# A fused attention and feed-forward kernel on one Trainium2 core: the order of the last four work units, the PSUM banks they use, and the last batch's feed-forward by halves

## The reference

```python
# x: (16, 256, 256) f32; 16 query heads, 4 key/value heads, head size 128
x = x + attn(layernorm(x))   # mask: k <= q and (k < 4 or k >= q - 31)
#   q = x @ wq.T; k = x @ wk.T; v = x @ wv.T; softmax(q k / sqrt(128)) v; then @ wo.T
x = x + ffn(layernorm(x))
#   w_q = round(weight / w_scale), per output row; x_q = round(x / x_scale), per token
#   y = (x_q @ w_q.T) * x_scale * w_scale + bias
```

## Time and profile before

| | us |
|---|---|
| median of three runs | 634.7 (633.99 to 635.71) |
| the profiled execution | 634.63 |
| its span, first to last instruction | 632.8 |
| PE busy | 599.3 (95%) |
| DVE busy | 544.8 (86%) |
| ACT busy | 399.7 (63%) |
| POOL busy | 307.8 (49%) |

### The profile page before, as it was taken

One profiled execution on the slowest core, in us unless ns is written; L12 is line 12 of the kernel. 1 busy time (PEld: TensorE's weight loads), 2 busy tenths in 40 slices (PEclk: granted clock), 3 DMA queues, 4 the chain that ended last, 5 costly groups with the idle time before them and its releaser, 6 DMA issues.

```text
span 632.8 us, 18148 instructions
## 1 busy us (share of the span) xinstructions
PE 599.3 (95%) x7589; PEld 529.5 (84%) x7589; DVE 544.8 (86%) x1084; ACT 399.7 (63%) x631; POOL 307.8 (49%) x302
## 2 busy tenths in 40 slices
PE   5759999999999999999999999999999999999983
PEld 4547888889898988989898888989898888989872
DVE  5876899989898988989898998989898998988885
ACT  5676766566666666666666666667666666665740
POOL 1142445464565546455554646456554745535440
PEclk9989999999999999999999999999999999999996
DMA  9931401213040311203040221304030120304000
GB/s 295 352 103 20 116 1 49 55 35 85 3 117 2 86 34 46 73 15 105 1 120 2 67 52 37 83 9 112 3 96 24 53 68 20 99 1 118 3 18 34
DMA packets 33841, 41.31 MB, mean 65 GB/s; under 512 B 3936, under 2 KB 24416, under 8 KB 33760
## 3 DMA queue, kind: packets, MB, share of 16 engines
q1 hardware_dynamic: 33616, 40.02, 22.9%
q10 hardware_dynamic: 144, 0.13, 0.1%
HBM read 10.26 MB, written 4.19 MB: 23 GB/s over the span
## 4 chain that ended last, share of the span: by engine, by line
PE 87%; DVE 7%; ACT 3%; issue 1%; POOL 1%; DMA 1%; POOLq 0%; SPq 0%; ACTq 0%
PE ps L551 26%; PE ps L429 25%; PE ps L456 7%; PE ps L396 7%; PE ps L405 6%; PE ps L512 5%; PE ps L533 4%; PE ps L534 4%; PE ps L384 1%; PE ps L578 1%; DVE WoT L1008 1%; DVE Qs L892 1%; PE ps L566 1%; PE ps L336 1%; DMA X<-in_L_attn_x 1%
## 5 line engine op out<-in xcount | busy, mean ns | idle before, releaser
L429 PE MATMUL ps<-xT,WqT 128*128 128x256 f16 x1536 | 178.2, 273 | 2.0 <-DVE WqT L1008 1.3
L551 PE MATMUL ps<-WoT,pool 128*128 128x256 f16 x1536 | 178.0, 273 | 0.2 <-DVE pool L916 0.2
L429 PEld LDWEIGHTS ps<-xT,WqT 128*128 128x128 f16 x1536 | 147.0, 98 | 19.1 <-issue 3.0
L551 PEld LDWEIGHTS ps<-WoT,pool 128*128 128x128 f16 x1536 | 147.5, 98 | 16.4 <-DVE pool L916 0.3
L1203 POOL TENSOR_TENSOR small<-E,rr 128x576 f32<-128x576 f32 x63 | 72.6, 1152 | 99.8 <-DVE rr L911 99.8
L775 ACT ACTIVATE pool<-ps 128x512 f16<-128x512 f32 x128 | 69.5, 595 | 81.7 <-PE ps L534 81.6
L1209 POOL TENSOR_TENSOR PP<-small,PP 128x576 f16<-128x576 f32 x63 | 80.9, 1284 | 68.2 <-ACT PP L768 68.2
L735 ACT ACTIVATE Qs<-ps 128x576 f16<-128x576 f32 x128 | 82.4, 644 | 43.6 <-PE ps L429 43.6
L1195 POOL TENSOR_TENSOR Sm<-Sm,mx 128x576 f32<-128x576 f32 x64 | 73.7, 1152 | 54.2 <-DVE mx L902 52.9
L892 DVE TENSOR_TENSOR Qs<-ps,Qs 128x576 f16<-128x576 f32 x128 | 92.6, 724 | 3.2 <-ACT Qs L735 3.0
L916 DVE SCALAR_TENSOR_TENSOR pool<-ps,pool 128x512 f16<-128x512 f32 x128 | 81.8, 680 | 0.8 <-ACT pool L775 0.8
(11 more groups left out here) (110 smaller groups left out, 888.0 us busy)
## 6 DMA issues: line engine op xcount, KB each, us to landing
VW<-Vn SPq DMA_DIRECT2D x48, 120.0 KB
big<-Vn SPq DMA_DIRECT2D x48, 120.0 KB
X<-in_L_attn_x SPq DMA_DIRECT2D x16, 256.0 KB, 7.7
VW<-VW SPq DMA_DIRECT2D x16, 256.0 KB, 3.2
big<-big SPq DMA_DIRECT2D x16, 256.0 KB, 3.4
out<-pool SPq DMA_DIRECT2D x15, 256.0 KB, 3.6
big<-in_L_attn_wq SPq DMA_DIRECT2D x4, 512.0 KB, 7.6
pool<-in_L_attn_wo SPq DMA_DIRECT2D x4, 512.0 KB, 9.1
```

The source lines that it names most:

```text
L429: a = pe.matmul(banks[BANK_Q[f]][:, j * 256:j * 256 + 256], WqT[:, k, wl, h * 128:h * 128 + 128], xT[:, b % 2, k, xl, :], start=(n == 1), ...
L551: a = pe.matmul(banks[BANK_OUT][:, t * 256:t * 256 + 256], OT[:, p, ol, h, t * 128:t * 128 + 128], WoT[:, 4 * g + h, wl, :], start=first, ...
```

## The change

Nothing changes in the loop except that `out_proj` of unit 59 leaves its last pass. Behind the loop:

- PE: after the scores of 62 come the queries of 63 and only then `pv` of 60; `out_proj` of 59 stands behind the scores of 63; the transposes of 63 stand directly behind those of 62.
- PSUM: `pv` of units 61 and 63 writes to the queries' banks 0 and 1. The last batch's `out_proj` writes its second row tile to bank 3, so that each tile has a bank; its matmuls go tile by tile, and in unit 63 each tile signals for itself. The feed-forward of batches 13 to 15 uses banks 6, 2 and 4.
- DVE: the last batch's residual, statistics, normalisation, quantisation and output go by tiles of 128 rows. The output of batch 14 and both additions of the bias leave DVE.
- ACT: two scaled copies make batch 14's output, and the last transpose is evacuated by halves.
- POOL: it takes both additions of the bias to x, the multiplication of batch 14's output by the weight scales and its last addition, and the reciprocal roots by tiles.

```diff
@@ -242,16 +243,32 @@
-def o_view(j):
-    return banks[BANK_O[j]][:, :].rearrange("p (h q) -> p h q", h=4), slice(128 * j, 128 * j + 128)
-def f_bank(b):
-    return BANK_KV if b == B - 1 else BANK_F
+def o_bank(u, j):
+    return (BANK_Q if u in (NU - 3, NU - 1) else BANK_O)[j]
+def o_view(u, j):
+    return banks[o_bank(u, j)][:, :].rearrange("p (h q) -> p h q", h=4), slice(128 * j, 128 * j + 128)
+def out_view(b, t):
+    if b == B - 1:
+        return banks[(BANK_OUT, BANK_F)[t]][:, 0:256]
+    return banks[BANK_OUT][:, t * 256:t * 256 + 256]
+def xq_view(b, t):
+    bank = {B - 2: BANK_PT, B - 1: (BANK_KV, BANK_O[0])[t]}.get(b, BANK_F)
+    return half(bank, BF16)[:, 0:512].rearrange("p (k t) -> p k t", k=2)[:, :, t * 128:t * 128 + 128]
+def fm_view(b, t):
+    bank = {B - 3: BANK_KV, B - 2: BANK_PT, B - 1: (BANK_KV, BANK_O[0])[t]}.get(b, BANK_F)
+    return banks[bank][:, t * 256:t * 256 + 256]
...
-    return {NU - 3: BANK_KV, NU - 1: BANK_KV}.get(u, BANK_PT)
+    return BANK_KV if u == NU - 3 else BANK_PT
@@ -314,10 +331,10 @@
-    sp.wait_ge(f_z, 2)
+    sp.wait_ge(f_zp, 2)
...
-    sp.wait_ge(f_z, 3)
+    sp.wait_ge(f_z, 1)
@@ -504,7 +521,7 @@
-            pe.wait_ge(pt_ok, u - 1)
+            pe.wait_ge(pt_ok, u)
@@ -520,7 +537,13 @@
             pe.wait_ge(vw2[j][b % 2], 16 * (b // 2 + 1))
-        if u:
+        if u == NU - 3:
+
+            pe.wait_ge(q_l, 2 * (NU - 1) + j + 1)
+        elif u > NU - 3:
+
+            pe.wait_ge(o_l, 2 * u + j - 3)
+        elif u:
@@ -543,12 +566,26 @@
+        if b == B - 1:
+            if g == 0:
+                pe.wait_ge(s_m, NU)
+            for t in range(2):
+                for h in range(4):
+                    for n, (ol, wl) in enumerate(PAIRS):
+                        a = pe.matmul(out_view(b, t), OT[:, p, ol, h, t * 128:t * 128 + 128], WoT[:, 4 * g + h, wl, :],
+                                      start=(g == 0 and h == 0 and n == 0), stop=(g == KV - 1 and h == 3 and n == 2),
+                                      skip_group_check=True)
+                if t == 0 and g == KV - 1:
+                    a.then_inc(out_ps, 1)
+            a.then_inc(out_ps, 1)
+            return
...
-                    a = pe.matmul(banks[BANK_OUT][:, t * 256:t * 256 + 256], OT[:, p, ol, h, t * 128:t * 128 + 128],
+                    a = pe.matmul(out_view(b, t), OT[:, p, ol, h, t * 128:t * 128 + 128],
@@ -557,26 +594,45 @@
-            pe.wait_ge(f_y, 2 * b)
-        elif b < B - 2:
+            pe.wait_ge(pt_ok, NU)
+        else:
...
-        v = half(f_bank(b), BF16)[:, 0:512].rearrange("p (k t) -> p k t", k=2)
-        for k in range(2):
-            for t in range(2):
-                a = pe.transpose(v[:, k, t * 128:t * 128 + 128], xq[:, t, k * 128:k * 128 + 128], idb[:, :])
+        for t in range(2):
+            for k in range(2):
+                a = pe.transpose(xq_view(b, t)[:, k, :], xq[:, t, k * 128:k * 128 + 128], idb[:, :])
...
-        if b < B - 2:
-            pe.wait_ge(s_m, 4 * b + 11 if b < B - 3 else NU)
+        if b < B - 3:
+            pe.wait_ge(s_m, 4 * b + 11)
+        elif b == B - 3:
+            pe.wait_ge(pt_ok, NU - 2)
...
-                a = pe.matmul(banks[f_bank(b)][:, t * 256:t * 256 + 256], xqT[:, k, t * 128:t * 128 + 128],
-                              WfT[:, k, :], start=(k == 0), stop=(k == 1))
+                a = pe.matmul(fm_view(b, t), xqT[:, k, t * 128:t * 128 + 128], WfT[:, k, :], start=(k == 0), stop=(k == 1))
+        a.then_inc(fm_ps, 1)
+    def ffn_last(t):
+        pe.wait_ge(f_xq, B + t)
+        if t == 0:
+            pe.wait_ge(f_y, 2 * (B - 2))
+        else:
+            pe.wait_ge(o_l, 2 * (NU - 1))
+        for k in range(2):
+            a = pe.transpose(xq_view(B - 1, t)[:, k, :], xq[:, t, k * 128:k * 128 + 128], idb[:, :])
+        a.then_inc(ft_ps, 1)
+        pe.wait_ge(f_t, B + t)
+        for k in range(2):
+            a = pe.matmul(fm_view(B - 1, t), xqT[:, k, t * 128:t * 128 + 128], WfT[:, k, :], start=(k == 0), stop=(k == 1))
@@ -659,7 +715,7 @@
-        if back:
+        if back and t < NU - 3:
@@ -669,29 +725,30 @@
     scores(u)
+    q_fill(u + 1, 0)
+    q_fill(u + 1, 1)
     pv(u - 2, 0)
     pv(u - 2, 1)
-    q_fill(u + 1, 0)
-    q_fill(u + 1, 1)
     p_transpose(u - 1)
     scores(u + 1)
-    out_proj(u - 2)
-    ffn_mm(B - 3)
+    out_proj(u - 3)
     pv(u - 1, 0)
     pv(u - 1, 1)
+    ffn_mm(B - 3)
+    out_proj(u - 2)
     p_transpose(u)
+    p_transpose(u + 1)
     pv(u, 0)
...
     out_proj(u - 1)
-    p_transpose(u + 1)
     pv(u + 1, 0)
...
     ffn_mm(B - 2)
-    ffn_t(B - 1)
-    ffn_mm(B - 1)
+    ffn_last(0)
+    ffn_last(1)
@@ -754,8 +811,22 @@
-        act.activation(xqT[:, :, :], half(f_bank(b), BF16)[:, 0:512].rearrange("p (k t) -> p k t", k=2),
-                       ACT.Copy).then_inc(f_t, 1)
+        src = bass.AP(ps, 512 * (BANK_PT if b == B - 2 else BANK_F), [[4096, 128], [1, 256]]).bitcast(BF16)
+        act.activation(xqT[:, :, :], src.rearrange("p (k t) -> p k t", k=2), ACT.Copy).then_inc(f_t, 1)
+    def ffn_last_t_evac(t):
+        act.wait_ge(ft_ps, B + t)
+        if t == 0:
+            act.wait_ge(fm_ps, B - 1)
+        act.activation(xqT[:, :, t * 128:t * 128 + 128], xq_view(B - 1, t), ACT.Copy).then_inc(f_t, 1)
+    def ffn_scaled(b):
+        act.wait_ge(fm_ps, b + 1)
+        act.wait_ge(f_o, 2 * b - 1)
+        for t in range(2):
+            act.activation(y[:, t, :], fm_view(b, t), ACT.Copy, scale=fx[b % 2][:, 2 + t:3 + t]).then_inc(f_ya, 1)
@@ -834,26 +905,28 @@
     p_high(u - 1)
+    q_high(u + 1, 0)
+    q_high(u + 1, 1)
+    exps(u)
     o_high(u - 2, 0)
     o_high(u - 2, 1)
-    q_high(u + 1, 0)
-    exps(u)
-    q_high(u + 1, 1)
     pt_evac(u - 1)
...
     o_high(u - 1, 1)
+    p_high(u + 1)
     pt_evac(u)
-    p_high(u + 1)
+    pt_evac(u + 1)
     o_high(u, 0)
     o_high(u, 1)
-    pt_evac(u + 1)
     o_high(u + 1, 0)
...
     ffn_t_evac(B - 2)
-    ffn_t_evac(B - 1)
-    act.wait_ge(f_z, 4)
+    ffn_scaled(B - 2)
+    ffn_last_t_evac(0)
+    ffn_last_t_evac(1)
+    act.wait_ge(f_z, 2)
     act.dma_start(out_v[B - 1][:, 1, :], yo[:, (B - 1) % 2, 1, :]).then_inc(out[(B - 1) % 2], 16)
@@ -952,29 +1025,51 @@
-    def with_bias(b):
-        dve.wait_ge(ld_b, 16)
-        dve.wait_ge(f_x2, b + 1)
-        dve.wait_ge(out[b % 2], 16 * (b // 2))
-        dve.tensor_tensor(yo[:, b % 2], X[:, 2 * b:2 * b + 2, :], brow[:, :].unsqueeze(1).to_broadcast([128, 2, D]),
-                          ALU.add).then_inc(f_xb, 1)
...
-        if b == B - 1:
-            dve.wait_ge(f_z, 2)
-        elif b:
+        if b:
...
-        if b >= B - 2:
-            dve.wait_ge(f_xb, 2)
...
-            dve.scalar_tensor_tensor(y[:, t, :], banks[f_bank(b)][:, t * 256:t * 256 + 256], fx[b % 2][:, 2 + t:3 + t],
+            dve.scalar_tensor_tensor(y[:, t, :], fm_view(b, t), fx[b % 2][:, 2 + t:3 + t],
...
-            if b >= B - 2:
-                dve.wait_ge(f_y, 2 * b + t + 1)
-                dve.tensor_tensor(yo[:, b % 2, t, :], yo[:, b % 2, t, :], y[:, t, :], ALU.add).then_inc(f_z, 1)
+    def last_residual(t):
+        x2 = X[:, 2 * (B - 1) + t, :]
+        dve.wait_ge(out_ps, NU + t)
+        dve.scalar_tensor_tensor(x2, out_view(B - 1, t), osc[:, 0:1], x2, ALU.mult, ALU.add).then_inc(f_x2, 1)
+        dve.wait_ge(f_x2, B + t)
+        dve.bn_stats(st2[:, t, :], x2).then_inc(f_st, 1)
+        dve.wait_ge(f_st, 4 * (B - 1) + 2 * t + 1)
+        dve.bn_aggr(mv2[:, t, :], st2[:, t, :]).then_inc(f_st, 1)
+    def last_quant(t):
+        f, n = fx[(B - 1) % 2], 3 * (B - 1 + t)
+        dve.wait_ge(f_rs, 2 * (B + t))
+        dve.tensor_scalar(xn2[:, t, :], X[:, 2 * (B - 1) + t, :], mv2[:, t, 0:1], rs2[:, t, 0:1],
+                          ALU.subtract, ALU.mult).then_inc(f_xn, 1)
+        dve.wait_ge(f_xn, 2 * (B - 1) + t + 1)
+        dve.tensor_reduce(f[:, t:t + 1], xn2[:, t, :], AX.X, ALU.max, apply_absolute_value=True).then_inc(f_s, 1)
+        dve.wait_ge(f_s, n + 1)
+        dve.tensor_scalar(f[:, 2 + t:3 + t], f[:, t:t + 1], 1.0 / 127.0, 1e-12, ALU.mult, ALU.max).then_inc(f_s, 1)
+        dve.wait_ge(f_s, n + 2)
+        dve.reciprocal(f[:, 4 + t:5 + t], f[:, 2 + t:3 + t]).then_inc(f_s, 1)
+        dve.wait_ge(f_s, n + 3)
+        dve.tensor_scalar(xr[:, t, :], xn2[:, t, :], f[:, 4 + t:5 + t], MAGIC, ALU.mult, ALU.add).then_inc(f_xr, 1)
+        dve.wait_ge(f_xr, 2 * (B - 1) + t + 1)
+        dve.wait_ge(ft_ps, B - 1)
+        dve.tensor_scalar(xq[:, t, :], xr[:, t, :], MAGIC, 127.0, ALU.subtract, ALU.min).then_inc(f_xq, 1)
+    def last_out(t):
+        dve.wait_ge(fm_ps, B + t)
+        dve.wait_ge(f_xq, B + t)
+        dve.scalar_tensor_tensor(xr[:, t, :], fm_view(B - 1, t), fx[(B - 1) % 2][:, 2 + t:3 + t],
+                                 wsrow[:, :], ALU.mult, ALU.mult).then_inc(f_y, 1)
+        dve.wait_ge(f_y, 2 * (B - 2) + t + 1)
+        dve.wait_ge(f_xb, 2)
```

(49 more changed lines are left out.)

## The result

The changed kernel takes 633.3 us in the median of 12 runs (632.95 to 633.93), where the kernel before took 635.1 (633.97 to 636.48) in 12 runs of the same occasions: ratio 0.9973, 95% interval 0.9963 to 0.9982. That is 1.75 us less, with an interval from 1.1 to 2.3. I had predicted 633.2, with the span 1.4 shorter, and put the line between faster and the same at a fall of 1.9 (0.3%). The measured fall stays just short of that line.

A forecast was written before the change was run, and what follows sets the result against it. PE's matmuls (87% busy) bound the kernel, then a serial end. PE ending at 618.9 and the reworked end cut the span 1.4, from 632.8 to 631.4; the profiled execution's 634.63 against the median 634.7 gave 633.2, range 630.8 to 635.0.

The forecast's parts named there:

- The units on PE: Last units on PE: scores of 62 start 0.95 us earlier, scores of 63 1.9 earlier, the moved projection covering 63's softmax.
- PE's gain: Up to the last projection: idle time 3.4 us against 4.4, so PE gains 1.0 and ends at 618.9.
- The idle stretches: PE's gaps among the last units: 1.67 us before the scores of 62, 1.1 between the transposes of 62 and 63.
- The 0.5 for the last projection's wait: Last projection waits 0.5 us for `o_low` of 63, queued behind batch 14's norm on DVE beside three POOL operations.
- The port: In the end, DVE's SBUF-to-SBUF `tensor_scalar` operations stand still while POOL works through a large tile; second xq at 626.75.
- Rival 1: In the end, the second tile's norm gets in before POOL's third operation, xq 1.1 us earlier: 632.1; chance 0.25.
- Rival 2: PE gains nothing, idle one more microsecond before the projection of 60: 634.2; chance 0.11.
- Rival 3: No wait at the port DVE and POOL share, so quantisation runs through: 629.9; chance 0.10.
- Rival 4: PE's clock falls to 1.2 GHz in the 1.67 us gap and the last three projections double: 641; chance 0.06.
- The halves of PE, ACT and DVE operations: One tile's operations in the end, sized from whole ones: transposes 0.44, evacuation 0.42, matmuls 0.64, together 1.5 us.
- Batch 14's output: Its DVE work before the change, put at 0.90 us, lay in PE's shadow and was free.
- up to here the split has cost 0.4: In the end, the second tile's xq comes at 626.75, where both tiles had theirs at 626.37 before.

The follow-up runs named there:

- late_bias14: `early_bias` with POOL scaling batch 14's output after the first tile's xq, DVE's attention additions later, and batch 14's bias after its xq: 631.1 us, ratio 0.9947.
- proj_back: Changed kernel with the projection of unit 59 back in front of the scores of 62: 634.3 us, tail 0.71 longer.
- old_order: Changed kernel with the old order of the last units on PE, ACT and DVE, keeping new banks and new end: 634.8 us, tail 0.88 longer.
- old_end: Changed kernel with batch 15's norm and quantisation for both tiles together, and bias and batch 14's output back on DVE: 631.9 us, ratio 0.996.
- early_bias: Changed kernel with POOL adding batch 15's bias and x early, near 607, and DVE adding the attention by tiles: 632.5 us, ratio 0.9969.
- joint: Changed kernel with norm, maximum and quantisation of batch 15 for both tiles together: 633.7 us, tail 0.87 longer.

## Why the prediction was right, and where its terms were off

Counted from unit 61's exponential, the prediction's steps against the measured ones (us):

| step | predicted | measured |
|---|---|---|
| scores of 62 start | 2.73 | 2.86 |
| scores of 63 start | 7.63 | 7.96 |
| last projection ends | 27.6 | 27.99 |
| second tile's statistics end | 28.7 | 29.17 |
| roots done | 29.8 | 30.15 |
| POOL's last operation ends | 33.7 | 33.99 |
| second tile's xq ends | 35.4 | 35.70 |
| last DVE operation ends | 37.9 | 38.21 |

- **The units on PE: right in kind, 0.4 too good.** The term that is off is PE's gain, put at 1.0 and measured at 0.61. The idle stretches were put at 1.67 and 1.1 and are 1.79 and 1.21. Matmuls behind a gap also cost PE about 0.16 more, which I had left out: the scores of 62 count for 0.95 in the chain after a gap and for 0.79 behind a running projection, whose end covers their first 0.16. By the scores of 63 this makes 0.33 of the 0.4. The 0.5 for the last projection's wait was about right: moving the third POOL operation away brought 0.42.
- **The port: right.** Rounding, xq and the second tile's norm ended 0.15 to 0.16 behind POOL's three operations. The 128x1 operation did not meet one of them here; where it did, in `late_bias14`, it passed. The run without those operations shows the 2.8 us. The runs with POOL's work moved in time show that it is the overlap that costs, not the work. The Trainium skill ("SBUF — State Buffer", section "Who interferes with whom") calls it one port pair held by whichever operation issues first; the trace agrees, with 1.19 us for an operation of 0.35.
- **Rival 1** (the norm gets in before POOL's third operation) did not come: the norm started at 623.43 and POOL's at 623.44 by the timeline, and POOL went through (1.26) while the norm took 1.42. POOL won in all three profiles in which the two started within 0.01 us of each other (this one, `proj_back` and `old_order`).
- **Rival 2**: PE did not wait before the projection of 60. **Rival 3**: excluded by the 1.2 us operations. I had put it 3.3 below the forecast; without POOL's work the end is 2.8 shorter, and the norm of batch 14 adds 0.42. **Rival 4**: the clock stayed at 1.00 to 620, through a gap of 1.79.
- **The halves of PE, ACT and DVE operations** were sized well: 0.44, 0.42 and 0.64 predicted from whole ones, 0.43, 0.44 and 0.64 measured with handovers (626.42 to 627.98 is 1.56, predicted 1.5); the maximum 0.42 (0.45 predicted), xq 0.29 (0.33). Batch 14's output was 1.8 us of DVE work in the kernel before (626.27 to 628.06), not 0.90; as all of it lay in PE's shadow, the sum stays the same.
- The median fell by 1.75 us, 0.7 more than the tail. The profiled executions had reached unit 61's exponential at 590.6 to 591.7 in kernels that are the same up to there, so the start varies by 1.1 us from one execution to the next. Whether the changed kernel's start is also earlier on average is not settled by these runs; the interval of the fall begins at 1.1, just above the tail's 1.05. That the median came out within 0.12 us of the forecast is partly luck: the tail lost 0.35 of the 1.4 that I had forecast for it, and a difference outside it made up for that.

What I had not seen: I counted the contention as part of the forecast, and never asked whether the new end was worth having. My own working gave xq at 626.75 where it had been 626.37, "up to here the split has cost 0.4"; counted from the last projection's end it was 7.85 in place of 6.45, so the split had cost 1.4. The old end behind the new order was a sum I could have made from the same rows. Without the 0.5 of waiting it gives 618.4 + 10.66 = 629.1 (an estimate), no worse than my 629.2. `old_end`, which keeps some of the work by tiles, took 9.3 in place of the 10.66.

## What to carry to other kernels

Moving elementwise work from DVE to an idle POOL can lengthen DVE's path: while POOL works through a large tile, DVE's SBUF-to-SBUF `tensor_scalar` operations stand still for the rest of it. Before moving such work, list the DVE operations of that kind beside it, and put POOL's part where DVE reads PSUM or reduces (0.86 for two `with_attention` in `early_bias` and 0.42 for the maximum in `late_bias14`, both beside POOL and not lengthened), or make it wait for the critical operation. A change of several parts that gains a little should be taken apart: here the kernel without two of the parts has a tail 2.4 us shorter than before, and those two together give 1.3 of it back, though one of them, the tiles, is a gain.

## What the runs showed of the hardware

- A DVE `tensor_scalar` of 128x256 between SBUF tensors took 0.35 us alone and 1.19 beside a POOL `tensor_tensor` of 128x512; the same kind on 128x1 took 0.15 beside it (`late_bias14`), and on 128x2 it was held (0.46 in place of 0.17, `joint`). Three such POOL operations in a row held three DVE operations in a row, one each.
- POOL can be the one that is held: its addition of 128x1 took 0.59 beside a DVE addition of two SBUF tensors, 0.19 without.
- The reciprocal root (`pow`) on POOL took 0.56 us for one element a row and 0.70 for two.
- 27 matmuls behind an idle stretch of PE took 0.95 us from the stretch's end; behind running matmuls the same group added 0.79.
